# Summing the softmax in ScalarE's second exponential, head by head, in place of a column of ones in the product with the values

## The reference

```python
# layer 0: W1 = W2 = adj, so C - A is the bias alone
h = jnp.maximum(_layernorm(x), 0.0)
x = x + max over n of relu(A + (C - A)),  A = adj @ h,  C = A + b
# layer 1: attention over the 128 nodes, 8 heads of 64
h = jnp.maximum(_layernorm(x), 0.0)          # x of layer 0's output
q, k, v = h @ Wq + bq, h @ Wk + bk, h @ Wv + bv
scores = q @ k.T / sqrt(64) + where(adj == 0, -1e9, 0)
weights = softmax(scores)
x = x + weights @ v
```

## Time and profile before

| | us |
|---|---|
| median of 3 runs | 1316.65 (1316.41 to 1317.42) |
| the profiled execution | 1314.74 |
| its span, first to last instruction | 1313.0 |
| TensorE busy | 1283.2 (98%) |
| VectorE busy | 1056.3 (80%) |
| GpSimd busy | 1028.8 (78%) |
| ScalarE busy | 945.6 (72%) |
| the second exponential (L460), 127 of 1024 columns | 132.1, 1.040 each |
| product with the values (L951), 3,024 matmuls | 114.1 |

### The profile page before, as it was taken

One profiled execution on the slowest core, in us unless ns is written; L12 is line 12 of the kernel. 1 busy time (PEld: TensorE's weight loads), 2 busy tenths in 40 slices (PEclk: granted clock), 3 DMA queues, 4 the chain that ended last, 5 costly groups with the idle time before them and its releaser, 6 DMA issues.

```text
span 1313.0 us, 30866 instructions
## 1 busy us (share of the span) xinstructions
PE 1283.2 (98%) x11193; PEld 670.7 (51%) x11193; DVE 1056.3 (80%) x2217; ACT 945.6 (72%) x1451; POOL 1028.8 (78%) x1165
## 2 busy tenths in 40 slices
PE   6999999999999999999999999999999999999995
PEld 3455555555555555555555555555555555555553
DVE  7588788788788888888888888887887887888777
ACT  6877777777777777777777777777777777777665
POOL 5887877887887888788788778778778778878665
PEclk9999999999999999999999999999999999999998
DMA  6366566566555555555555655655665665664344
GB/s 201 67 137 137 123 143 133 127 138 136 130 132 142 131 124 145 135 121 146 137 122 138 139 127 134 137 133 127 139 137 121 141 142 121 136 144 116 89 89 112
DMA packets 435237, 171.68 MB, mean 131 GB/s; under 512 B 400528, under 2 KB 400656, under 8 KB 435088
## 3 DMA queue, kind: packets, MB, share of 16 engines
q1 hardware_dynamic: 433744, 169.46, 56.2%
q10 hardware_dynamic: 1344, 0.27, 0.1%
HBM read 37.03 MB, written 33.55 MB: 54 GB/s over the span
## 4 chain that ended last, share of the span: by engine, by line
PE 94%; DVE 3%; ACT 1%; issue 1%; POOL 0%; DMA 0%; POOLq 0%; DVEq 0%; ACTq 0%
PE proj L892 50%; PE proj L910 24%; PE sc L928 7%; PE proj L951 7%; PE proj L875 6%; DVE shifted L634 0%; DVE w L744 0%; DVE masked L622 0%; DVE row_max L626 0%; DMA x_in<-in_x 0%; ACT qk L442 0%; POOL probs L343 0%; DVE q_peaks L756 0%; ACT h L429 0%; ACT qkT L440 0%
## 5 line engine op out<-in xcount | busy, mean ns | idle before, releaser
L892 PE MATMUL proj<-hT,w 128*128 128x512 f16 x3072 | 706.1, 380 | 2.3 <-DVE hT L796 2.0
L892 PEld LDWEIGHTS proj<-hT,w 128*128 128x128 f16 x3072 | 295.6, 98 | 357.3 <-issue 3.6
L336 POOL TENSOR_TENSOR qkT<-qk,qkT 128x512 f16<-128x512 f32 x256 | 315.7, 1233 | 66.9 <-ACT qk L442 66.4
L910 PE MATMUL proj<-w,hT 128*128 128x512 f16 x1536 | 352.2, 379 | 0.4 <-DVE v L611 0.3
L343 POOL TENSOR_TENSOR probs<-probs 128x1024 f16<-128x1024 f32 x127 | 271.2, 2136 | 21.7 <-ACT probs L460 21.5
L458 ACT ACTIVATE probs<-shifted 128x1024 f16<-128x1024 f32 x127 | 134.3, 1057 | 181.3 <-DVE shifted L634 181.2
L440 ACT ACTIVATE qkT<-proj,bqk_up 128x512 f16<-128x512 f32 x256 | 173.5, 678 | 102.7 <-PE proj L892 102.7
L611 DVE SCALAR_TENSOR_TENSOR v<-proj,v 128x512 f16<-128x512 f32 x128 | 88.4, 691 | 162.9 <-ACT v L448 162.9
L910 PEld LDWEIGHTS proj<-w,hT 128*128 128x128 f16 x1536 | 141.6, 98 | 152.4 <-DVE v L611 0.7
L634 DVE TENSOR_TENSOR shifted<-masked,row_max 128x1024 f32<-128x1024 f32 x127 | 207.7, 1635 | 2.3
L656 DVE SCALAR_TENSOR_TENSOR y<-proj,out_scale,x 128x64 f32<-128x64 f32 x992 | 201.7, 277 | 4.6 <-DVE out_scale L645 0.3
(11 more groups left out here) (84 smaller groups left out, 1023.5 us busy)
## 6 DMA issues: line engine op xcount, KB each, us to landing
x_in<-in_x SPq DMA_DIRECT2D x128, 256.0 KB, 3.0
out_x<-y SPq DMA_DIRECT2D x128, 256.0 KB, 2.4
probsT<-probs SPq DMA_TRANSPOSE x127, 3.7
hT<-h SPq DMA_TRANSPOSE x124, 3.1
w_raw<-in_L_gnn_Wq SPq DMA_DIRECT2D x4, 256.0 KB, 7.4
w_raw<-in_L_gnn_Wk SPq DMA_DIRECT2D x1, 1024.0 KB, 9.3
w_raw<-in_L_gnn_Wv SPq DMA_DIRECT2D x1, 1024.0 KB, 11.6
bv_rows<-in_L_gnn_bv ACTq DMA_DIRECT2D x1, 256.0 KB, 7.2
```

The costliest lines, as they stand in the source:

```text
L336: pool.tensor_tensor(qk_place(k, u, 1), qk32[:, u % 2, :], qk_place(k, u, 0), ALU.subtract).then_inc(qk_rest_done, 1)
L892: last = nc.tensor.matmul(proj[:, QK_BANKS[u % 2], :], w16[:, j, s, c, col * P:(col + 1) * P], hT[:, k // GROUP % HT_GROUPS, t, c, :, :].r ...
L910: last = nc.tensor.matmul(v_bank(m), hT[:, m // GROUP % HT_GROUPS, s, c, k % GROUP, :], w16[:, 2, t, c, :], start=(c == 0 and i == 0), sto ...
```

## The change

ScalarE's second exponential is split into its eight heads of 128 columns, and each of the eight ACTIVATEs also hands out the sum of what it writes, into a new tile `sums` (four elements deep, in the order of heads of `probs`). VectorE scales and inverts these sums (`out_scale_of`), now after `probs_done` and not after the product; the multiply-adds wait for the product themselves. The column of ones goes: `v16` has 64 places a head without gaps, all matmuls of the product are 64 columns wide, and the whole product of an element is 512 columns, one bank (`o_head`: bank 2 of `proj`; `sc` bank 0 for element 124; for the last element `sc` banks 2 and 3, by halves). With this `probs_times_v` no longer waits for `qk_evac`, and the even chunk no longer for `y_low_done`, which is gone. No instruction changes its place among the others of its engine.

```diff
-        v16 = sb("v16", [P, 2, GROUP, H, VP], F16)
+        v16 = sb("v16", [P, 2, GROUP, H, HD], F16)
...
+        sums = sb("sums", [P, GROUP, H])
+        scaled_sum = sb("scaled_sum", [P, H])
+        out_scale = sb("out_scale", [P, GROUP, H])
...
+        def place(h):
+
+            return h % 2 * HALF + h // 2
+
+        def o_head(m, h):
+
+            if m == B - 1:
+                return sc[:, 2 + h % 2, h // 2 * HD:h // 2 * HD + HD]
+            bank = sc[:, 0, :] if m == B - 4 else proj[:, O_HIGH, :]
+            return bank[:, place(h) * HD:place(h) * HD + HD]
...
                     wait(act, probs_rest_done, m)
-                    nc.scalar.activation(probs[:, :, :], shifted[:, :, :], ACT.Exp, scale=HD ** -0.5).then_inc(probs_done, 1)
+                    wait(act, sum_done, m - GROUP + 1)
+                    for h in range(H):
+                        last = nc.scalar.activation(probs[:, h, :], shifted[:, h, :], ACT.Exp, scale=HD ** -0.5,
+                                                    accum_out=sums[:, k % GROUP, h:h + 1])
+                    last.then_inc(probs_done, 1)
...
             def out_scale_of(m, count):
 
-                if m >= B - 4:
-                    dve.wait_ge(y_scaled, m - B + 5)
-                dve.wait_ge(o_ready, m + 1)
-                nc.vector.tensor_scalar(scaled_sum[:, :, :], o_view(m)[:, :, :, HD], redo[:, 2:3], None,
-                                        ALU.mult).then_inc(sum_done, 1)
+                if m == B - 2:
+                    dve.wait_ge(y_scaled, 1)
+                dve.wait_ge(probs_done, m + 1)
+                nc.vector.tensor_scalar(scaled_sum[:, :], sums[:, m % GROUP, :], redo[:, 2:3], None, ALU.mult).then_inc(sum_done, 1)
                 dve.wait_ge(sum_done, count)
-                nc.vector.reciprocal(out_scale[:, m % 2, :, :], scaled_sum[:, :, :]).then_inc(out_scale_done, 1)
+                nc.vector.reciprocal(out_scale[:, m % GROUP, :], scaled_sum[:, :]).then_inc(out_scale_done, 1)
...
                     dve.wait_ge(out_scale_done, count or m + 1)
+                    dve.wait_ge(o_ready, m + 1)
...
-            nc.vector.memset(v16[:, 0, :, :, HD:VW].rearrange("p g h e -> p (g h) e"), 1.0).then_inc(mask_done, 1)
...
                     wait(pe, qk_evac, 2 * (base + k) - 1 + u % 2)
-                    if u % 2 == 0:
-                        wait(pe, y_low_done, base + k - Y_BEHIND)
...
                     pe.wait_ge(v_evac, m + 1)
-                    wait(pe, qk_evac, min(2 * (m + OUT_BEHIND) + 1, 2 * B))
...
-                            w = HD if t else VW
-                            last = nc.tensor.matmul(o_view(m)[:, h % 2, h // 2, 0:w], probsT[:, k % 2, s, h % 2 * 4 + h // 2, :],
-                                                    v16[:, t, k % GROUP, h, 0:w],
+                            last = nc.tensor.matmul(o_head(m, h), probsT[:, k % 2, s, place(h), :],
+                                                    v16[:, t, k % GROUP, h, :],
                                                     start=(i == 0), stop=(i == 2))
```

## The result

The changed kernel takes 1430.52 us (1430.24 to 1431.26, 4 runs) against 1316.53 us: a ratio of 1.0864, 95% interval 1.0851 to 1.0877. The profiled execution took 1430.40 us with a span of 1428.6. Slower was forecast, with 1470 us in a range of 1388 to 1600. So the direction held, and the bound moved where it was said to; the loss of 114 us is three quarters of the 153 us forecast.

The account below looks back on a forecast made before the run. TensorE bounded the kernel before; with the change, a ring of ScalarE and VectorE work would. 1314.74 + 149 for the loop + 4.4 for the tail = 1468 us on the profiled run's clock, so 1470 us, range 1388 to 1600.

Parts of the forecast that it names:

- The bound moves to a ring with the second exponential in it: ScalarE and VectorE's closed sequence from v_head through shift, both exponentials, evacuations and add_c to next v_head; replaces TensorE as bound.
- room in the ring: Slack of ScalarE and VectorE's closed sequence against TensorE's 19.86 us in two elements: 1.09 us before the change.
- 18.77 us of own work in two elements: Work from one v_head to that two slots on, without the wait for TensorE: 8.90 odd, 9.87 even.
- X: Time the change adds to ScalarE's second exponential in each element, forecast as 2.72 - 0.95 = 1.77 us.
- Who comes last at the shift: VectorE's shift before the exponentials: 1.39 us odd, 1.89 even, by how GpSimd's work falls beside it.
- A head at 0.20 without its sum: One 128-column ACTIVATE of ScalarE's second exponential: 0.09 fixed plus 0.11 us for columns; eight are 1.60.
- The store at r = 0.14: Second small ScalarE instruction storing each head's sum, priced 0.14 us, between 0.09 and 0.19; bounded by nothing and 0.28.
- 1418 us: Forecast kernel time if each sum's store on ScalarE costs 0.09 us, one column by the skill's page.
- Waits added, 0: Second exponential's wait for an older scaling and VectorE's scaling's wait for an exponential: both long past, cost 0.
- The product with the values, 0: TensorE's 16 fewer columns in 24 instructions: 0.9 us in all if TensorE stayed the bound, taken as 0.
- What is late next: Transposed probabilities reach TensorE later; it waits about 1.22 us in every slot, but this adds no second term.
- TensorE's clock: Stays at 1.00 despite waits each slot; rival at 1.2 GHz gives over 2,400 us, chance 0.03.

Follow-up runs that it names:

- the split alone: Kernel before, with its second exponential cut into eight ACTIVATEs of 128 columns and no sums: 1336.92 us, ratio 1.015.
- the sums beside the column of ones: Kernel before, second exponential cut into eight, each also handing out a sum nobody reads; column of ones, two banks and waits stay: 1429.98 us, ratio 1.0858.

## Why the prediction was right, point by point

- **The bound moves to a ring with the second exponential in it.** Right, and shown from three sides: adding 0.65 us to it costs 20 us, taking 0.61 out of it (add_c) gives 58 back, taking 1.75 out gives 91 back and puts TensorE at the head of the chain again (63%); on the kernel before, with room in the ring, the same 1.75 gives nothing.
- **18.77 us of own work in two elements.** Right as a number: 20.13 measured for 20.07, and 21.60 for 21.55 with the X that was measured. The shift of the even slot takes 2.01 us by the loop's median where the earlier trace rows have 1.89.
- **Who comes last at the shift.** Here the prediction's ring is not the whole story, and that its sum came out is in part luck. It took the shift's 1.39 and 1.89 for work whose length depends on how GpSimd's work falls beside it. They are for the most part a wait inside the instruction, which no semaphore shows. This is the even slot of the changed kernel:

```profile
670.27 2.13 POOL L351 TENSOR_TENSOR probs<-probs 128x1024 f16<-128x1024 f32 x1 [0.71 <-ACT probs L470]
672.36 1.16 POOL L344 TENSOR_TENSOR qkT<-qk,qkT 128x512 f16<-128x512 f32 x1
673.48 1.27 POOL L336 TENSOR_TENSOR x<-x,bv_rows 128x512 f32<-128x512 f32 x1
674.72 1.15 POOL L328 TENSOR_TENSOR h<-h 128x512 f16<-128x512 f32 x1
675.83 1.15 POOL L344 TENSOR_TENSOR qkT<-qk,qkT 128x512 f16<-128x512 f32 x1
676.05 2.02 DVE L651 TENSOR_TENSOR shifted<-masked,row_max 128x1024 f32<-128x1024 f32 x1
```

  GpSimd's last instruction here ends at 676.98, and the shift 1.09 later, at 678.07. So it is everywhere: in 125 of the 127 elements of the changed kernel, and in 123 of 127 before, a GpSimd instruction was running when the shift began, and the shift ended 1.08 after it by the median; where none was running it took 1.22 in all. And in the changed kernel, in all 116 elements of the loop's middle, GpSimd had worked without a break since the second exponential released it. So a second path closes beside the one that was forecast: the second exponential, GpSimd's queue, the shift, the two exponentials. v_head and add_c are not on it, the 1.39 us are, and so the sum is the same by either. The two meet in whether the shift begins behind four of GpSimd's instructions or five. Moving add_c made it begin earlier, behind four (at 731.92, with the fourth at work from 731.18 to 732.35): the even slot fell from 11.36 to 10.24 and the odd one stayed at 10.24 by the medians. That is 1.1 in two elements, not 1.22. No run changed GpSimd's own work, so what it would be worth there is not shown.
- **A head at 0.20 without its sum.** Right: in the split alone the ACTIVATEs of 128 columns start 0.20 apart, and with sums the store starts 0.20 after its ACTIVATE.
- **The store at r = 0.14.** The term that was mis-sized. It is 0.09 (0.187 long, and the next ACTIVATE starts 0.093 after it by the median), the lower of the two values between which the forecast was put, that of an instruction which doesn't wait for the end of the one ahead. X is 1.39 and not 1.77: 122 x 0.38 = 46 us too much in the forecast. The Trainium skill's page "ScalarE: Activation LUTs", section "What ACT_TABLE_LOAD costs", gives 186 ns fixed and an overlap of about 93 ns for an ACTIVATE. The trace agrees for the store too, with 187 ns and 0.093 us from start to start, so the prediction's estimate from that page, 1418 us, is the nearer one.
- **What is left, 1430 against 1418.** From the first v_head to that of element 122 the trace has 107 us more than before (from 66.90 to 1383.24, before from 64.08 to 1273.05), against 101 by the sum at r = 0.09; this is the difference between 21.60 and the sum's 21.51 for two elements, and between 19.85 and 19.86 before. The tail has 5.5 more, against 3. And the first v_head is 2.8 later, which the forecast had left out and no run explains.
- **Waits added, 0.** Right in the loop, not in the tail. There the second exponential's new wait for a scaling was not past: `DVE scaled_sum L659` held it twice, for 0.93 at 1395.03 (L470) and for 1.35 at 1413.84 (the last element's, L571). VectorE had queued the scaling behind its shift, and the scaling, 0.20 long in the loop, took 1.50 and 2.09 there. Both times it ended 0.03 after a GpSimd instruction that ran beside it:

```profile
1411.18 2.63 POOL L351 TENSOR_TENSOR probs<-probs 128x1024 f16<-128x1024 f32 x1 [2.44 <-ACT probs L470]
1411.74 2.09 DVE L659 TENSOR_SCALAR scaled_sum<-sums,redo 128x8 f32<-128x8 f32 x1
1413.84 0.31 ACT L571 ACTIVATE probs<-shifted 128x128 f32<-128x128 f32 x1 [1.35 <-DVE scaled_sum L659]
```

  So that VectorE's scaling "keeps its size" was wrong in the tail. These waits are not the most of the tail's 5.5: without them, with the sums beside the column of ones, it is still 4.7.
- **The product with the values, 0.** Wrong in size, by 3.6 us for a TensorE that is the bound, where 0.9 was the most that was allowed. With 64 columns in place of 65 and 64, all in one bank, the 24 take 0.89 and not 0.92. Since in the changed kernel TensorE isn't the bound, this didn't show in its time. Whether it is the width, the bank or the places without gaps was not tried.
- **What is late next.** Right that late transposes add nothing in the changed kernel. Wrong that TensorE waits for them in every slot: its loads do so in 37 of 127 elements, and it waits for VectorE's v_rest in 87 (39.5 us). Once the ring is out of the way, at 1340 us, its loads wait for transposes in 23 to 26 elements; what part of the last 23 us this is was not shown.
- **TensorE's clock.** It was granted 1.00 from 100 to 1300 us, as forecast. TensorE had 75.5 us without work in that stretch, 1.9 us at most at a time.

No version here that computes the reference beats the kernel before. The bank's gain of 3.6 us was seen only without the sums on ScalarE.

## What to carry to other kernels

A bound at 94% of the chain says nothing on the distance to the next one. Look for a wait that is there in one slot and missing in the next, follow the ring of engines that closes there, and add up its own work from start to start: 18.77 of 19.86 us was all the warning there was. Work put into such a ring costs its full length once the room is used up. The same work on the same engine costs far less where the order of instructions keeps it out of the ring: moving v_head ahead of 1.75 us of other work gave back four fifths of the loss. Look also for an instruction that is longer than its own kind elsewhere, as the shift is here with 2.01 against 1.22 us: it may be waiting for another engine where no semaphore and no idle time shows it. A sum handed out by an ACTIVATE is an instruction of its own, so eight short pieces with sums cost 2.34 us where one long one costs 0.95.

## What the runs showed of the hardware

- A ScalarE instruction ACTIVATION_READ_ACCUMULATOR stands behind each ACTIVATE with a sum: 187 ns by the median, 0.09 us from its start to the next ACTIVATE's, 1,016 of them between 185 and 194 ns long.
- The transposing DMA of the probabilities takes 3.7 us from issue to landing by the median, in the kernels before and after alike, and up to 5.6 before, 6.0 after and 6.1 with v_head moved. What makes some of them long was not found.
- VectorE's shift (fp32, both inputs in SBUF) takes from 1.21 us to 3.09 us for the same 1,024 columns. Begun while a GpSimd TENSOR_TENSOR runs, it ends 1.08 us after that one, in all 123 such elements of the kernel before; begun while none runs, it takes 1.22 us. Then it is GpSimd that is held: with the shift begun at 1391.79, GpSimd's L351, begun at 1391.83, took 3.17 us in place of 2.13.
- VectorE's scaling of eight sums takes 0.19 to 0.23 us when it reads PSUM, whatever GpSimd does (129 of 129 in the kernel before). Reading SBUF it takes 0.20 to 0.22 alone, and up to 2.09 beside a GpSimd instruction, then ending 0.03 us after it by the median (126 cases with v_head moved).
